# Last stage of an audio tower on one core: the stacked operands loaded by six DMAs instead of twelve, and one group of transposes moved in TensorE's order

## What is computed

```
sx = einsum('bsh,ndh->bnsd', x, hl_w) + hl_b
q = einsum('bnsd,neod->bneso', sx, wq);  k, v = the same with wk, wv
att = softmax(einsum('bnesd,bntd->bnest', q, k) * d ** 0.5 + causal)
qkv = where(pad, 0, einsum('bnest,bntd->bnesd', att, v))
mixed = sum over the experts of qkv, weighted by a softmax gate
hn = layernorm(mixed + resid)                 # the "mixed heads" (fx)
hx = relu(hn @ fc1.T + b) -> @ fc2.T + b -> layernorm -> gate -> out
```

## Time and profile before

| | us |
|---|---|
| median of three executions | 3402.48 |
| lowest and highest | 3365.5, 3409.38 |
| the profiled execution | 3390.36 |
| span of its trace | 3388.6 |

### The profile page before, as it was taken

How to read it: one execution, slowest core, us unless ns; L and a number is a source line. 1 busy time by engine, 2 the same in 40 slices (tenths; PEclk the granted TensorE clock), 3 DMA queues, 4 the chain that set the end, 5 groups by cost and what they waited for, 6 DMA issues and landing times.

```text
span 3388.6 us, 81043 instructions
## 1 busy us (share of the span) xinstructions
PE 3081.6 (91%) x24964; PEld 2193.7 (65%) x24964; DVE 2615.6 (77%) x7699; ACT 1817.5 (54%) x4484; POOL 1301.8 (38%) x1368
## 2 busy tenths in 40 slices
PE   0699999999999899998999998999999999999995
PEld 0588888888888634444777776666666666666663
DVE  4788888888888578886888865788777777778773
ACT  0355555555555445554766643555555555555552
POOL 1443444434344144441000022445445444444432
PEclk9999999999999989997888867999889989989996
DMA  4100000000000000000000013443333333333420
GB/s 140 35 22 22 14 21 14 21 20 15 21 14 8 1 1 0 0 0 1 1 0 0 0 28 58 71 66 64 59 59 59 58 59 60 70 57 63 68 36 4
DMA packets 74280, 110.98 MB, mean 33 GB/s; under 512 B 20105, under 2 KB 65481, under 8 KB 73577
## 3 DMA queue, kind: packets, MB, share of 16 engines
q1 hardware_dynamic: 72936, 106.85, 16.9%
q10 hardware_dynamic: 1024, 0.39, 0.0%
HBM read 76.01 MB, written 30.82 MB: 32 GB/s over the span
## 4 chain that ended last, share of the span: by engine, by line
PE 25%; issue 9%; POOL 6%; DMA 6%; DVE 5%; SPq 2%; ACT 1%; POOLq 0%; DVEq 0%; ACTq 0%
DMA qe_K<-query_key_parts 4%; PE psum L2329 3%; PE psum L1660 3%; PE psum L2315 2%; PE psum L2343 2%; POOL qe_root L3032 2%; PE psum L2302 2%; DMA query_key_parts<-qe_parts 2%; PE psum L2366 2%; PE psum L1689 2%; PE psum L1677 1%; SPq L2221 1%; PE psum L1731 1%; SPq L2223 1%; POOL qe_parts L3014 1%
## 5 line engine op out<-in xcount | busy, mean ns | idle before, releaser
L2782 DVE TENSOR_REDUCE qe_top<-psum 125x1 f32<-125x375 f32 (+2 forms) x896 | 500.8, 596 | 238.1 <-PE psum L2302 235.7
L2589 ACT ACTIVATE qe_E<-psum 125x375 f32<-125x375 f32 (+1 forms) x896 | 459.0, 531 | 285.1 <-PE psum L2302 261.0
L2302 PE MATMUL psum<-bconst 125*125 125x125 bf16 (+2 forms) x1792 | 491.3, 274 | 0.0
L625 PE MATMUL psum<-Q,K 96*125 96x125 f32 (+3 forms) x2304 | 404.5, 311 | 0.5 <-ACT E L836 0.4
L2315 PE MATMUL psum<-qe_K,qe_Q 96*125 96x375 bf16 (+2 forms) x1536 | 332.0, 300 | 59.4 <-DMA qe_K<-query_key_parts 32.3
L625 PEld LDWEIGHTS psum<-Q,K 96*125 96x125 f32 (+1 forms) x2304 | 334.3, 189 | 24.5 <-issue 1.2
L2329 PE MATMUL psum<-qe_Q,qe_K 97*125 97x375 bf16 (+2 forms) x1536 | 336.8, 299 | 2.4 <-ACT qe_E L2589 2.0
L1175 POOL TENSOR_TENSOR Q<-rot 64x375 f32<-64x375 f32 (+1 forms) x256 | 305.7, 1213 | 73.4 <-DVE rot L976 61.4
L836 ACT ACTIVATE E<-psum 125x500 f32<-125x500 f32 x384 | 226.2, 589 | 172.7 <-PE psum L645 169.5
L2315 PEld LDWEIGHTS psum<-qe_K,qe_Q 96*125 96x125 bf16 x1536 | 182.4, 148 | 167.1 <-DVE qe_top L2782 71.6
L2302 PEld LDWEIGHTS psum<-bconst 125*125 125x125 bf16 x1792 | 266.4, 149 | 9.8 <-issue 6.9
(11 more groups left out here) (341 smaller groups left out, 7199.7 us busy)
## 6 DMA issues: line engine op xcount, KB each, us to landing
qe_Q<-query_key_parts SPq DMA_DIRECT2D x192, 187.5 KB, 6.2
query_key_parts<-qe_parts SPq DMA_DIRECT2D x32, 843.8 KB, 3.6
s_row<-scores SPq DMA_DIRECT2D x32, 366.2 KB
qe_K<-query_key_parts SPq DMA_DIRECT2D x192, 46.9 KB, 6.6
x_tokens<-x SPq DMA_DIRECT2D x32, 187.5 KB
x_chunks<-x SPq DMA_DIRECT2D x4, 750.0 KB
E<-x SPq DMA_DIRECT2D x4, 750.0 KB
out<-qe_hout SPq DMA_DIRECT2D x32, 93.8 KB
```

The source lines that it names most:

```text
L625: nc.tensor.matmul(out[:, first * TP:(first + n) * TP].rearrange("p (o q) -> p o q", o=n), t.K[0:rows(h), par, h, jt * TP:(jt + 1) * TP], ...
L2302: return nc.tensor.matmul(out, B("ident_b")[0:TP, 0:TP], rhs, start=False, stop=True, skip_group_check=True)
L2589: nc.scalar.activation(E[:, e % 2, a:a + width], bank[0:TP, 4 + n % 2, 0:width], ACT.Exp).then_inc(e_done, 1)
L2782: nc.vector.tensor_reduce(dst, src, AX, ALU.max).then_inc(m_read, 1)
```

## The change

The twelve loads of the stack become six: the 96 rows are grouped as runs of 48, 32 and 16 rows. In each run the first 3, 2 or 1 parts of Q are paired with part 0, 1 or 2 of K; the pairs are the same six as before, in another order of rows. For a run to be one DMA the scratch is laid out anew (queries first, then keys), the columns of the projection weights are permuted, and the store becomes two DMAs, one of queries, one of keys. A run of K repeats the same 16 rows 3, 2 or 1 times. Bytes that are loaded and stored stay the same.

Second, `turn_mixed` moves from between exp22 and exp23 to behind max0 of the next round, and `keep_mixed` on ScalarE from before to behind the exponential of exp23.

```diff
@@ weight_layout
-    heads = z(D, 4, HE, 2, DH2)
+    queries, keys, values = z(D, 2, DH2, HE, 2), z(D, 1, DH2, 2, HE), z(D, 1, HE, 2, DH2)
     for n in range(HE):
         rows = slice(n * DH2, (n + 1) * DH2)
         for e in range(EE):
-            heads[rows, e % 2, n, e // 2] = l["wq"][n, e].T
-        heads[rows, 2, n, 0] = l["wk"][n].T
-        heads[rows, 3, n, 0] = l["wv"][n].T
+            queries[rows, e % 2, :, n, e // 2] = l["wq"][n, e].T
+        keys[rows, 0, :, 0, n] = l["wk"][n].T
+        values[rows, 0, n, 0] = l["wv"][n].T
@@ query_experts
-    q_parts, k_parts = (0, 0, 1, 0, 1, 2), (0, 1, 0, 2, 1, 0)
-    RS = len(q_parts) * DH2
+    RUNS = (3, 2, 1)
+    RS = sum(RUNS) * DH2
@@ sync, stack
-                sp.dma_start(qk_dram, parts[:]).then_inc(parts_stored, 16)
+                sp.dma_start(queries.rearrange("p r s -> r p s"), parts[:, :, 0:2, :].rearrange("r p i s -> r p (i s)")
+                             ).then_inc(parts_stored, 16)
+                sp.dma_start(keys.rearrange("p r s -> r p s"), parts[:, :, 2, :]).then_inc(keys_stored, 16)
                 sp.wait_ge(parts_stored, (b + 1) * 16)
-                for g, (qp, kp) in enumerate(zip(q_parts, k_parts)):
-                    rows = slice(g * DH2, (g + 1) * DH2)
-                    sp.dma_start(Q[rows, slot].rearrange("d (a i) s -> d a i s", i=2), rows_of[qp, :, :, 0:2]
-                                 ).then_inc(stacked, 16)
-                    sp.dma_start(K[rows, slot], keys_of[0, kp, 2]).then_inc(stacked, 16)
+                sp.wait_ge(keys_stored, (b + 1) * 16)
+                at = 0
+                for kp, n in enumerate(RUNS):
+                    rows = slice(at, at + n * DH2)
+                    sp.dma_start(Q[rows, slot].rearrange("d q s -> d (q s)"), query_rows[0:n * DH2]).then_inc(stacked, 16)
+                    sp.dma_start(K[rows, slot].rearrange("d h s -> d (h s)"),
+                                 key_rows[kp:kp + 1, :, 0:HE * S].to_broadcast((n, DH2, HE * S))).then_inc(stacked, 16)
+                    at += n * DH2
@@ tensor, step
                 if on[2]:
                     scores_for_max(bs[2], s[2], 0)
+                if on[5]:
+                    turn_mixed(bs[5], s[5])
+                if on[2]:
                     scores_for_max(bs[2], s[2], 1)
...
-                if on[4]:
-                    turn_mixed(bs[4], s[4])
@@ scalar, step
-                if on[4]:
-                    keep_mixed(bs[4], s[4])
                 if on[3]:
                     exponentials(bs[3], s[3], 23)
+                if on[4]:
+                    keep_mixed(bs[4], s[4])
```

More of the change, by code:

```diff
@@ L215, in weight_layout @@
         for e in range(EE):
-            heads[rows, e % 2, n, e // 2] = l["wq"][n, e].T
-        heads[rows, 2, n, 0] = l["wk"][n].T
-        heads[rows, 3, n, 0] = l["wv"][n].T
-    k.add("w_heads", heads.reshape(D, 4, 128))
+            queries[rows, e % 2, :, n, e // 2] = l["wq"][n, e].T
+        keys[rows, 0, :, 0, n] = l["wk"][n].T
+        values[rows, 0, n, 0] = l["wv"][n].T
+    k.add("w_heads", np.concatenate([v.reshape(D, -1, 128) for v in (queries, keys, values)], 1))
     gw = z(128, EE, HE * EE)
@@ L2178, in query_experts @@
         folded, set_up, p_ready, v_ready, nz_ready, nz_done, v_kept = map(sem, ("folded", "set_up", "p", "v", "nz", "nz_done", "v_kept"))
-        hi_done, full_done, parts_done, parts_stored, stacked = map(sem, ("hi", "full", "parts", "parts_stored", "stacked"))
+        hi_done, full_done, parts_done, parts_stored, keys_stored, stacked = map(
+            sem, ("hi", "full", "parts", "parts_stored", "keys_stored", "stacked"))
         m_ready, m_read, neg_ready, neg_turned, maxT_kept = map(sem, ("m", "m_read", "neg", "neg_turned", "maxT"))
@@ L2208, in sync @@
         def sync(sp):
-            rows_of = qk_dram.rearrange("(a d) p i s -> p d a i s", d=DH2)
-            keys_of = qk_dram.rearrange("(h a d) p i s -> a p i d h s", a=2, d=DH2)
+            NQ = NP * 128 * 2 * S
+            queries = qk_dram[0:NQ].rearrange("(p r s) -> p r s", p=NP, r=128)
+            keys = qk_dram[NQ:].rearrange("(p r s) -> p r s", p=NP, r=128)
+            query_rows = queries.rearrange("p (d a) s -> (p d) (a s)", d=DH2)
+            key_rows = keys.rearrange("p (d h) s -> p d (h s)", d=DH2)
             def stack(b, slot):
                 wait(sp, e_ready, (b - 2) * NU)
-                wait(sp, stacked, b * 32 * len(q_parts))
+                wait(sp, stacked, b * 32 * len(RUNS))
                 sp.wait_ge(parts_done, (b + 1) * NP)
-                sp.dma_start(qk_dram, parts[:]).then_inc(parts_stored, 16)
+                sp.dma_start(queries.rearrange("p r s -> r p s"), parts[:, :, 0:2, :].rearrange("r p i s -> r p (i s)")
+                             ).then_inc(parts_stored, 16)
+                sp.dma_start(keys.rearrange("p r s -> r p s"), parts[:, :, 2, :]).then_inc(keys_stored, 16)
                 sp.wait_ge(parts_stored, (b + 1) * 16)
-                for g, (qp, kp) in enumerate(zip(q_parts, k_parts)):
-                    rows = slice(g * DH2, (g + 1) * DH2)
-                    sp.dma_start(Q[rows, slot].rearrange("d (a i) s -> d a i s", i=2), rows_of[qp, :, :, 0:2]
-                                 ).then_inc(stacked, 16)
-                    sp.dma_start(K[rows, slot], keys_of[0, kp, 2]).then_inc(stacked, 16)
+                sp.wait_ge(keys_stored, (b + 1) * 16)
[6 more added lines that the diff above has]
+                    at += n * DH2
             def store(b, slot):
@@ L2309, in scores_for_max @@
                 if n == 0:
-                    pe.wait_ge(stacked, (b + 1) * 32 * len(q_parts))
+                    pe.wait_ge(stacked, (b + 1) * 32 * len(RUNS))
                 if n == 2 and isinstance(b, int) and b == 0:
@@ L2565, in first_part @@
                     wait(act, parts_stored, b * 16)
+                    wait(act, keys_stored, b * 16)
                 nc.scalar.copy(parts[:, 0, i, :], bank[:, in_bank(b, i), 0:S]).then_inc(hi_done, 1)
@@ L2700, in step @@
                     exponentials(bs[3], s[3], 22)
+                if on[3]:
+                    exponentials(bs[3], s[3], 23)
                 if on[4]:
                     keep_mixed(bs[4], s[4])
-                if on[3]:
-                    exponentials(bs[3], s[3], 23)
                 if on[2]:
@@ L3111 @@
     out = nc.dram_tensor("out", (nb, S, D), F32, kind="ExternalOutput").ap()
-    qk_dram = nc.dram_tensor("query_key_parts", (128, 3, 3, S), BF16).ap()
+    qk_dram = nc.dram_tensor("query_key_parts", (128 * 3 * 3 * S,), BF16).ap()
     s_dram = nc.dram_tensor("scores", (nb * CI, TP), F32).ap()
```

## The result

| | median us | runs | ratio to before, 95% |
|---|---|---|---|
| before | 3392.16 | 4 (3365.5 to 3409.38) | |
| after | 3479.86 | 4 (3475.82 to 3501.99) | 1.028 (1.019 to 1.037) |

The change costs some 88 us. The prediction had 3322, and its range ended at 3405. The profiled execution took 3479.57 us, span 3477.8.

What follows compares the result with a forecast made beforehand. The prediction saw the last stage bound by TensorE, with idle waits and slow clock after late stacks. Gains of 25 + 2.5 + 1 + 52, about 80 us, off the 3402.48 median gave 3322 us, range 3290 to 3405.

Steps and rivals of the forecast that it cites:

- The value of an early stack: Last stage, TensorE before the turn of the maxima: waits for a late stack mostly go, gain 25 us, plus 52 us of clock.
- VectorE as the next bound: Undisturbed rounds of the last stage: turn_max is already bound by VectorE's negated maxima, following turn_mixed by 1.66 us.
- the 0.4 us before exp23: Last stage after the move: TensorE waits 0.4 us before exp23 for exp21's exponential, which ends near 2448.8.
- the 0.5 to 0.8 us for the negated maxima: Before the turn of the maxima: TensorE waits some 0.7 us; as a sign, 0.5 to 0.7 us in most rounds.
- the seven falls behind issue waits that stay: At the loop's jump back: the clock falls behind each of seven issue waits, and these falls stay.
- I take 9.4 ... 2.3 us less than 11.7: Stack loads: six loads of Q and K flow in 9.4 us instead of 11.7; with the store, landing at T + 16.0.
- The store's term: Store split in two with smaller pieces: +0.5 us taken, within bounds of 0 and +1.5 us.
- 5.5 us for Q and 1 to 2 for K: Stack loads, if K were spread over all sixteen DMA engines: 5.5 us for Q and 1 to 2 for K.
- In the undisturbed rounds the move is worth 0.1 us at most, and costs nothing: turn_mixed behind max0: 0.76 us wait goes, 0.4 + 0.7 comes, same end; 2.5 us gained in seven issue-wait rounds.
- that no second idle time is added to a late stack's: Larger use claimed for moving turn_mixed behind max0: TensorE's wait for mixed heads no longer adds to that for a late stack.
- Rival (c): Stack lands later, K serial on one engine; at 2.5 us later, 55 + 70 us lost, 3527 us; chance 0.08.
- I take it that the ten falls behind loads go: TensorE's clock in the last stage: ten falls behind waits for loads vanish, eight at 5.4 us, two at 4.3: 52 us.

Runs made afterwards that it cites:

- e12: Changed kernel plus ten more matmuls of 375 columns each round, ahead of the wait for the stack, results overwritten: 3343.02 us, ratio 0.988 to the kernel before.
- e4: Changed kernel with each run's rows ordered (row of the head, copy) instead of (copy, row), same six loads: 3321.44 us, ratio 0.9815 to the kernel before.
- e6: e4 without the move, turn_mixed and keep_mixed in their old places: 3323.54 us, ratio 0.982 to the kernel before.
- e8: e4 with the run of 32 rows back in the change's order (copy, row): 3419.24 us, ratio 1.012 to the kernel before.
- e3: Kernel before with only the move of turn_mixed behind max0 and of keep_mixed; store and twelve loads unchanged: 3440.7 us, ratio 1.020.
- e2: Changed kernel with turn_mixed and keep_mixed back in their old places: 3455.12 us, ratio 1.022 to the kernel before.
- e10: e4 with Q's loads issued once the queries are stored, K's after the keys' store: 3306.61 us, ratio 0.977 to the kernel before.
- e11: e10 with turn_mixed directly behind exp23 instead of behind max0: 3308.66 us, ratio 0.976 to the kernel before.
- e13: e10 with turn_mixed in its old place: 3312.47 us, ratio 0.977 to the kernel before.
- e7: Kernel before with turn_mixed moved only past exp23, so between exp23 and max0, and keep_mixed behind exp23's exponential: 3385.92 us, ratio 0.999.
- e14: Kernel before with ten more matmuls of 375 columns each round ahead of the wait for the stack: 3331.13 us, ratio 0.985.
- e5: Changed kernel's scratch and split store, but twelve loads of 16 rows, nothing repeated, pieces of 12000 and 3000 bytes: 3457.45 us, ratio 1.022 to the kernel before.

## Why the prediction was wrong

**What held.** The bound was read rightly: a stack that lands late costs its wait and, behind it, a slow round; e12 shows the second part to be the larger. The value of an early stack was right in kind: e4 and e6 have a pass of three rounds at 116 us for 115. That they also end at 3321 and 3324 us for the forecast 3322 is partly luck. The forecast took 80 us off a median of 3402; e4 is 62 us under the kernel before that ran beside it (3384), with 11 falls and not seven. Right as well were VectorE as the next bound, the 0.4 us before exp23, the 0.5 to 0.8 us for the negated maxima, and the seven falls behind issue waits that stay.

**First failed step: "I take 9.4 ... 2.3 us less than 11.7".** Landing was forecast at T + 16.0 and was T + 18.3 in the sequence shown, T + 19.1 in the median. The store's term was short by 0.6 us (1.07 for 0.5), and by 0.9 in the median. The rest is K. That it would ride on 3 and then 2 engines was seen, but the load on those engines was priced at 23 GB/s for each, from a stretch of the first stage. That window had only 5 engines at work. In the packet records of this sequence a 3000-byte piece takes 247 ns (median) up to T + 13.5, while most engines are busy, and 121 ns from T + 15.4 on, when two are; one of 12000 bytes takes 862 ns. So on an engine that is busy beside the others the rate is 12 to 14 GB/s, and 25 only in the tail. If the first two engines carry 16 + 16 + 1 pieces of K and 6 of Q each, they work for 33 x 0.227 (the median of all K pieces) + 6 x 0.862 = 12.7 us; data starts at T + 5.6, which makes T + 18.3, near the T + 17.8 at which the last piece ends. Of these 12.2 us of flow Q's six pieces are some 5.2, and K's 99 KB some 7, where the prediction had 4.3. The packet records do not name the engine, so the sum over one engine is worked out; that the two K loads are on 3 and 2 engines is in the increments of `stacked`, and e8 and e4 show what it costs. That the forecast missed by no more was helped by the time around the flow, 1.5 us for the 2.5 between its 11.7 and 14.2. The Trainium skill says the same of the cause, in "DMA: Bandwidth & Descriptors", "Why a DMA increments its semaphore by 16 and not by 1" (the slowest dimension sets the number of engines), and in "Rules for kernel authors" of that page it names a leading repeated dimension as the trap and a dimension of a multiple of 16 in front as the way out; after and e4 agree with both: 3 and 2 engines and a landing at T + 18.3 there, sixteen for every load and T + 16.5 here.

The wide rows were taken too well too, which the failure on K hides. With K on all engines the prediction had 5.5 us for Q and 1 to 2 for K; with the 2.5 us around the flow that is 9 to 10 us from the first load's issue. e4 has this form and needs 11.5, with data flowing from T + 6.5 to T + 15.5.

**Second failed step: "In the undisturbed rounds the move is worth 0.1 us at most, and costs nothing".** e3 has it at 57 us. The step counted microseconds until the turn of the maxima and came out even; it did not ask how long TensorE idles when the stack is a little late. It even named as the larger use of the move "that no second idle time is added to a late stack's". That is where it fails: the transposes stood ahead of the wait for the stack and filled 0.5 us of it; behind max0 they do not, and exp23 is done sooner, so the idle time ahead of max0 grows from 0.32 to 1.24 us, and the clock falls in rounds that had kept it (18 falls before, 26 in e3). Rival (c) had the fall of the clock in rounds that kept it before, and its bound of "about 1 us later" from which it decides; it got 0.08. What came is in the main its mechanism: the stack lands 1.1 us later in the median and no round keeps its clock. Its price was 125 us; the loads alone cost 71 (e2), the whole change 88. Seen from behind, with a landing uncertain by 2.5 us to the late side, and rounds that kept their clock with 0.76 and 0.32 us of idle time, the chance should have been several times that.

**"I take it that the ten falls behind loads go"** hung on the first step, and held where that was mended (e10).

**The difference in sum**, 89 us between the two profiled spans, 88 of them in the last stage. TensorE's idle time there grows by 22 us: +28.8 (DMA), +2.7 (issue), -21.8 (mixed heads) and +12.5 (exp23, 14.5 for 2.0). Its busy time grows by 66 us with the same work. That is the clock: from 2030 us to the end 475 us stand at 1.2 GHz for 314, and 161 us more are 63 us at 5.4 us for 13.7.

## What to carry to other kernels

When several small DMAs are merged by repeating a source, look at the outermost dimension of the pattern: put the rows outside and the copies inside, else a "larger" DMA may run on as few engines as there are copies, as with 3 and 2 here. When filler work is moved around a wait that cannot be kept short, look at what is left on TensorE's side to fill it, and at the clock behind it: one group of matmuls ahead of the wait for the last operand or behind it was worth 55 us here, and ten useless ones ahead of it 137. Whether the longest idle piece counts or the sum was not separated. The end of such a change is reached once the operand is early; then the place of the filler made no difference that could be measured (e4 and e6; e10, e11 and e13).

## What was not expected of the hardware

- A pause of TensorE of 1.24 us in one piece, after one of 0.43 us ahead of exp23, was followed by 1.2 GHz (e3), and 0.43 + 0.47 us on either side of exp23 and three transposes was not (e7); the falls went 18, 26, 17 (before, e3, e7), with waits for the stack of 32, 42 and 33 us. What the chip looks at in such a pause was not measured. The twelve kernels without the ten matmuls have 260 round ends without an issue wait, 111 of them with a fall near the turn of the maxima; the longest pause and the sum of the pauses sort these equally well.
- Adding 32 x 10 matmuls to a kernel whose TensorE is busy for 90% of the span made it 4% faster (e12 against after).
- At each of the seven issue waits at the loop's jump the clock falls in every one of the fourteen traces. With the ten matmuls right behind the wait, the stretches at 1.2 GHz there were 3.4 or 6.8 us (e12, e14) and not 10.2 or 13.7 as in the twelve others, so what follows a pause seems to bear on how long the slow stretch lasts. This was not varied further.
- A store cut from 128 pieces of 6750 bytes into 768 of 1500 and 750 cost 1.07 us at the first load's issue in the sequence shown and 1.4 in the median. The size of loaded pieces mattered little: the twelve loads of e5 with 12000 and 3000 bytes take 13.5 us in the median, those of before with 1500 and 750 bytes 14.4.
- A piece of 3000 bytes took 247 ns while most DMA engines were busy and 121 ns when two were, in one load sequence of the changed kernel.
